# Edge judging of a graph network: the turned first rows move from SBUF into a PSUM bank, and TensorE picks before it sends messages

## The reference

```python
e_feat = jnp.concatenate([x[rol], x[col], edge_attr], axis=-1)   # 96 features per edge
h = jax.nn.relu(e_feat @ W1 + b1)                                # W1: 96 x 64
v = h @ W2 + b2                                                  # W2: 64 x 32
x_cand = jax.ops.segment_max(v, col, num_segments=num_nodes)     # maximum per target node
return jnp.maximum(x_cand, x[:, -v.shape[-1]:])
```

## Time and profile before

| | before |
|---|---|
| median of 3 runs | 11685.94 us (11680.96 to 11694.03) |
| the profiled execution's own time | 11690.6 us |
| its span, first to last instruction | 11688.9 us |
| of it, the judging stage | about 3550 us (6217 to 9767) |
| mean granted TensorE clock over the span | 0.808 of full speed |
| busy over the span | PE 79%, DVE 72%, ACT 42%, POOL 61% |

### The profile page before, as it was taken

The page is one execution under the profiler, slowest core; times in us unless marked ns, Lnnn a source line. Parts: engine busy times, 40 slices in busy tenths (PEclk is TensorE's granted clock), DMA queues, the critical chain, the costliest instruction groups (busy, mean ns, idle before and its releaser), DMA issues. The chain is left out here.

```text
span 11688.9 us, 285628 instructions
## 1 busy us (share of the span) xinstructions
PE 9274.5 (79%) x108602; PEld 7299.8 (62%) x108602; DVE 8456.4 (72%) x14013; ACT 4944.3 (42%) x9502; POOL 7132.8 (61%) x6941
## 2 busy tenths in 40 slices
PE   3566666666666656999996889888998883999999
PEld 3565555555555546999993444444444441999999
DVE  5788888888888867878785555555555555787878
ACT  2556555555555544666661000000000000666666
POOL 6777777777777762323277777777777776131313
PEclk7555555555555558999998999999999996999999
DMA  6333333333333337999994333333333332999998
GB/s 111 98 107 112 106 109 109 105 109 106 109 109 107 109 82 260 372 353 364 348 355 105 74 74 77 77 75 75 74 76 78 75 75 53 360 348 343 356 344 323
DMA packets 959125, 1957.99 MB, mean 168 GB/s; under 512 B 315235, under 2 KB 556857, under 8 KB 958641
## 3 DMA queue, kind: packets, MB, share of 16 engines
q1 hardware_dynamic: 591481, 1673.77, 38.9%
q0 software_dynamic: 223488, 179.16, 9.9%
q10 hardware_dynamic: 144056, 103.79, 3.2%
HBM read 1577.86 MB, written 381.48 MB: 168 GB/s over the span
## 5 line engine op out<-in xcount | busy, mean ns | idle before, releaser
L208 POOL DMA_INDIRECT edge_rows<-table,edge_list x3136 | 2982.1, 951 | 1048.9 <-issue 1011.1
L1671 POOL DMA_INDIRECT judge_edges_src_rows<-table,judge_edges_ring x2752 | 2681.3, 974 | 838.6 <-issue 826.5
L756 PE MATMUL attend_and_count_counts<-attend_and_count_hot_hi,attend_and_count_hot_lo 128*128 128x98 bf16 x15680 | 1569.2, 279 | 1139.8 <-DVE attend_and_count_hot_lo L785 975.7
L1517 POOL DMA_INDIRECT x_sb<-slot_sums,last_slot x588 | 939.5, 1598 | 2413.2 <-DMA slot_sums<-propagate_norm_whole 1225.1
L756 PEld LDWEIGHTS attend_and_count_counts<-attend_and_count_hot_hi,attend_and_count_hot_lo 128*128 128x128 bf16 x15680 | 1209.2, 132 | 1501.5 <-issue 1029.4
L884 ACT CAST attend_and_count_stage<-attend_and_count_counts 128x392 uint8<-128x392 f32 x3920 | 1567.0, 519 | 222.5 <-PE attend_and_count_counts L756 217.4
L1780 PE MATMUL judge_edges_p_pick<-judge_edges_x_split,judge_edges_low_hot 128*128 128x384 bf16 (+1 forms) x9216 | 1559.7, 329 | 0.0
L785 DVE TENSOR_TENSOR attend_and_count_hot_hi<-attend_and_count_p_ramp,attend_and_count_key_hi 128x784 bf16<-128x784 bf16 x1960 | 1010.7, 557 | 547.7 <-ACT attend_and_count_key_lo L853 530.7
L1780 PEld LDWEIGHTS judge_edges_p_pick<-judge_edges_x_split,judge_edges_low_hot 128*128 128x128 bf16 x9216 | 901.6, 98 | 706.3 <-issue 98.5
L785 DVE TENSOR_TENSOR attend_and_count_hot_lo<-attend_and_count_p_ramp,attend_and_count_key_lo 128x1024 bf16<-128x1024 bf16 x1960 | 1259.3, 684 | 27.1
L1248 PE MATMUL propagate_norm_p_dense<-propagate_norm_split,propagate_norm_part 128*128 128x96 bf16 x24304 | 1097.0, 207 | 214.4 <-DVE propagate_norm_split L1344 183.3
(11 more groups left out here) (301 smaller groups left out, 15334.1 us busy)
## 6 DMA issues: line engine op xcount, KB each, us to landing
propagate_mean_raw<-matrix SPq DMA_DIRECT2D x372, 1568.0 KB, 8.8
propagate_norm_raw<-matrix SPq DMA_DIRECT2D x372, 1568.0 KB, 8.7
matrix<-attend_and_count_stage SPq DMA_DIRECT2D x245, 784.0 KB, 3.6
scan<-attend_and_count_out SPq DMA_DIRECT2D x196, 272.0 KB
edge_rows<-table,edge_list POOLq DMA_INDIRECT x3136
inject<-attend_and_count_zeros SPq DMA_DIRECT2D x49, 1024.0 KB, 4.7
judge_edges_dst_rows<-inject SPq DMA_DIRECT2D x195, 256.0 KB
judge_edges_attr_rows<-in_edge_attr_dram SPq DMA_DIRECT2D x195, 256.0 KB
```

Source lines behind the costliest of these rows:

```text
L208: nc.gpsimd.indirect_dma_start(out=S.edge_rows[:, u, g, j, :], out_offset=None, in_=D.table0[:, :], in_offset=rows_of(S.edge_list[:, u, g, ...
L756: last = nc.tensor.matmul(counts[:, bank, NH * k:NH * k + NH], hot_lo[:, u, slot, :], hot_hi[:, u, slot, :], start=True, stop=True)
L1517: nc.gpsimd.indirect_dma_start(out=S.x[:, h, :], out_offset=None, in_=D.slot_sums[0:j * BLOCK, :], in_offset=rows_of(S.last_slot[:, h:h + ...
L1671: nc.gpsimd.indirect_dma_start(out=src_rows[:, u, lane, :], out_offset=None, in_=D.table2[:, :], in_offset=rows_of(ring[:, u, lane:lane + ...
```

## The change

The scan of the target rows (L1817) has read `keep` and `firsts`, both from SBUF. Now `firsts` is a PSUM bank. The transpose L1814 writes it there. The messages have one bank instead of two, which is where the bank comes from. So `send(s)` waits for the scan of the maximum of step s-1, and no longer only for that of step s-2. And `pick(s+2)` stands in front of `send(s-1)` in a step of TensorE.

```diff
-    firsts = sb("firsts2", [P, CHUNK], f32)
...
-    p_msg = pb("p_msg", [P, 2, CHUNK], f32)
+    p_msg = pb("p_msg", [P, CHUNK], f32)
+    firsts = pb("p_firsts", [P, CHUNK], f32)
...
             def send(it, u):
                 here = it * RING + u
                 pe.wait_ge(rectified, here + 1)
-                await_count(pe, topped, here - 1)
+                await_count(pe, topped, here)
                 for half in range(HALVES):
-                    last = nc.tensor.matmul(p_msg[:, u % 2], w2[:, half], hidden[:, u % 2, half],
+                    last = nc.tensor.matmul(p_msg[:], w2[:, half], hidden[:, u % 2, half],
...
             def one(it, u):
                 lift(it, u)
+                if is_picked(*ahead(it, u, 2)):
+                    pick(*ahead(it, u, 2))
                 if not (isinstance(it, int) and it + u == 0):
                     send(*before(it, u, 1))
-                if is_picked(*ahead(it, u, 2)):
-                    pick(*ahead(it, u, 2))
...
-                nc.vector.tensor_tensor_scan(out=best[:, u % 2], data0=neg[:, u], data1=p_msg[:, u % 2],
+                nc.vector.tensor_tensor_scan(out=best[:, u % 2], data0=neg[:, u], data1=p_msg[:],
```

## The result

| | before | changed |
|---|---|---|
| median | 11685.94 us | 11632.32 us (11619.97 to 11639.75, 5 runs) |
| ratio to before, 95% interval | | 0.995 (0.9939 to 0.9962) |
| the profiled execution: its own time | 11690.6 us | 11632.32 us |
| its span | 11688.9 us | 11630.6 us |
| first to last gather of the judging stage | 3518.7 us | 3457.0 us |

The changed kernel is faster by 53.6 us by the medians and by 58.3 us between the two profiled executions. In a second measurement the medians are 11679.42 us before and 11629.98 us changed, 49.4 us apart (ratio 0.9961, 0.9947 to 0.9974). The forecast was 11625 us, with a range from 11608 to 11650.

The account below looks back on a forecast made before the run. GpSimd's issue of gathers was taken to bound the judging stage. Terms of -61.5 and +0.4 us summed to -61.1 us, giving 11629.5 us profiled and 11625 us for the median, range 11608 to 11650 us.

Parts of the forecast that it names:

- (1): Target scan's second input in PSUM: the held gathers on GpSimd's path go, one for one, -61.5 us.
- (2): VectorE's transpose L1814 into PSUM: between 0.9 and 2.0 us, hidden in front of waits, 0 us.
- (3): send's wait for one more maximum scan: 0 us; scan ends at 5.8 us, send begins at 14.4 or more.
- (4): TensorE's pick in front of send: select's wait mostly goes, flags' transfer about 1.5 us earlier, 0 us gained.
- (6): End of the judging stage: the last send waits for a scan, last turn back starts later, +0.4 us.
- (7): Other stretched gathers, nearly all beside make_hot's comparisons: 8 us now, change of -8 to +19 us, taken as 0.
- (5): TensorE does the same products, busy 15.9 us of a 17.5 us step, 91%; less idle time can only help.
- Rival C: Slower: TensorE becomes the bound through the one message bank, 19.1 us a step against 17.84, +240 us, 11930 us; chance 0.03.

Follow-up runs that it names:

- e4: Changed kernel with the first rows turned into SBUF and the target scan reading a zeroed PSUM bank instead: 11628.75 us, ratio 0.9951 to before.
- e5: Changed kernel with the first rows still turned into PSUM but the target scan reading a zeroed SBUF buffer: 11703.68 us, ratio 1.0017 to before.
- e3: Changed kernel with the scan of the maxima reading a zeroed SBUF buffer in place of the messages' PSUM bank: 11711.08 us, ratio 1.0027 to before.
- e9: Kernel before with only the one message bank and its wait, old TensorE order, first rows in SBUF: 11686.07 us, ratio 0.9998.
- e2: Changed kernel with TensorE's old order, send in front of pick; first rows in PSUM, one message bank: 11622.73 us, ratio 0.9952 to before.
- e8: Kernel before with only TensorE's new order, pick in front of send; two message banks, first rows in SBUF: 11706.79 us, ratio 1.0015.
- e1: Changed kernel with the first rows back in SBUF; one message bank and the new order stay: 11710.23 us, ratio 1.0021 to before.
- e10: e1 plus an unused 1,312-column sum on VectorE in every other step, in front of the maximum scan: 11694.03 us, ratio 1.0006 to before.
- e7: e6 with the mask comparison at the stage's start reading its ramp from the first rows' PSUM bank: 11616.12 us, ratio 0.9947 to before.
- e6: Changed kernel with the five operations splitting the node features moved ahead of VectorE's wait for row numbers: 11621.29 us, ratio 0.9952 to before.

## Why the prediction was right

The numbers in brackets are the prediction's own parts.

1. *GpSimd sets the step, not TensorE with its 89%.* Right: the gather span less the held time is one number in ten executions.
2. *61.5 us of held gathers go, one for one (1).* Right, and shown: the gather span fell by 61.7 us, and e4, e5 and e3 put the cause on the scan's second input. The inference in the Trainium skill's "SBUF — State Buffer", section "Who interferes with whom", that a VectorE operation that takes only the shared read port leaves descriptor writing alone, doesn't hold for transfers that read row numbers from SBUF: 141 were held in e5, 159 in e3. The rule of the same section on two SBUF inputs fits the runs. The prediction tells the rule for one input without the section's exception, the modes that use both ports: the cast of the earlier trace rows has one input and held the gather on to 6251.71 us, 0.13 us behind its end. The runs show which operands hold a gather; the port itself no trace shows.
3. *The transpose into PSUM: nothing on the path (2).* Right on the path. Its size was wrong: I bounded it by 0.9 and 2.0 us, and it takes 0.737.
4. *One message bank and its wait: nothing (3).* Right: e9 is at 0.9998 of before, and e2 needs no new order. The scan of the maximum ended up to 6.4 us after the start of the source turn somewhere in the stage before, not 5.8; the 14.4 us were still far off.
5. *The new order: nothing (4).* Right only beside the PSUM bank. In e8 and e1, with the first rows in SBUF, it costs 13.6 to 15.8 us of gather span. I had seen that it would shift the flags by 1.5 us and had judged only whether they would come late. I had not asked at what point of a gather the scan would then start, which with the hold in place has a price. In the changed kernel there is no held time left for it to change.
6. *The end: +0.4 us (6).* Right: 16.1 to 16.5 us.
7. *The other stretched gathers stay at 8 us (7).* Right: 8.5 us are left, beside the comparisons of `make_hot`. The bounds of that term were -8 and +19 us, so the middle was a guess that came out.
8. *TensorE at 91% (5).* 90%, at the same clock, and not the bound. Rival C's sum is loosely rounded: 8.2 + 1.7 + 8.1 and a wait of 1 us are 19.0 us, which makes 227 us more and not 240.

The median fell by 53.6 us and not by 61.1. In the two profiled executions the gather span fell by 61.7 us and the whole by 58.3. The 3.4 us between them lie outside the gathers: the first gather starts at 6226.09 before and at 6231.36 us after, though the stages up to it are the same, and what follows the last gather is 1.9 us shorter. The other 4.7 us are the distance of the profiled execution before from its median. I had taken the same distance off the changed kernel, whose profiled execution is its median. In the profiles of before, the changed kernel and e1 to e5 and e8 to e10 that point lies anywhere from 6213.6 to 6231.4 us. I had taken nothing for that scatter in the sum; the range had it. Whether a usual execution of the kernel before holds gathers for 61.5 us, its one profile can't show; e9, which should be alike, has 57.4. What stays open is what sets the point of a gather at which a scan starts, and so why the held time is 61.5 us in one order and 75.3 in another. The held times of the profiled runs move by some 5 us for kernels that should be alike (61.5 and 57.4; 76.1 and 75.3), and e10 went against the simple account by the flags' request.

## What to carry to other kernels

Where GpSimd issues indirect transfers all the time, look in its timeline for those that last longer than the shortest, and lay them beside VectorE's instructions: those that end a fixed time behind a VectorE instruction are candidates for being held by it. Here a VectorE instruction with two inputs in SBUF lost that hold when one input came from a PSUM bank, even a bank that VectorE filled itself: the second input in two scans, the first in the comparison of e7. While such a hold is left in place, moves elsewhere can change its cost without touching it, so take it out before judging the order of the rest. Here it only paid because GpSimd's gathers set the step.

## What the runs showed of the hardware that was not expected

- VectorE's turn of 128x512 fp32 with an output step of 16 columns takes 737 ns into a PSUM bank and 1004 to 1007 ns into SBUF, in kernels that differ in little else (the changed kernel and e5 against before and e4).
- The time by which a held gather ends behind the scan, known from the kernel before, is the same at another scan (159 gathers in e3, 0.75 to 0.76 us) and in the other orders (0.75 to 0.77 us in e1, e5, e8, e9 and e10). Behind the comparison of e6 it was 0.81 us (6245.58 to 6246.39).
- The order of TensorE's work changes GpSimd's time by 14 us (e8, one profiled execution of each) without any wait of GpSimd for it: the difference is in the held time, that is in the point of a gather at which VectorE's scan starts. By e9's profile, held times of kernels that should be alike differ by 4 us.
